# Raw edge blocks and source numbers fetched ahead of the gathers, kept in DRAM and brought back by SyncE

## What is computed

```python
edge_index = stack([src, dst])                  # 200,000 edges + one loop a node, sorted by dst
x = x + gnn(layernorm(x), edge_index, W, b, prelu_a)
x = x + ffn(layernorm(x)[None], Wr, br, W1, b1, W2, b2, gamma, beta)[0]

def gnn(x, edge_index, k_centers, W, b, prelu_a):
    deg = segment_sum(ones, dst); dinv = rsqrt(deg)
    h = x @ W
    out = segment_sum(h[src] * (dinv[src] * dinv[dst])[:, None], dst) + b
    return where(out > 0, out, prelu_a * out)
# ffn: 8 experts, the two best chosen once from the mean over all nodes, then for every node
#      gelu(x @ W1[e] + b1[e]) @ W2[e] + b2[e], weighted sum of the two, + x, layer norm
```

## Time and profile before

| | us |
|---|---|
| median of 3 runs | 1024.82 (1023.86 to 1029.19) |
| the profiled execution | 1025.88 |
| span of its core | 1024.4 |
| mean granted TensorE clock | 0.987 |

### The profile page before, as it was taken

How to read it: one execution, slowest core, us unless ns; L and a number is a source line. 1 busy time by engine, 2 the same in 40 slices (tenths; PEclk the granted TensorE clock), 3 DMA queues, 4 the chain that set the end, 5 groups by cost and what they waited for, 6 DMA issues and landing times.

```text
span 1024.4 us, 20188 instructions
## 1 busy us (share of the span) xinstructions
PE 981.2 (96%) x6916; PEld 831.5 (81%) x6917; DVE 845.5 (83%) x1737; ACT 508.5 (50%) x998; POOL 550.8 (54%) x510
## 2 busy tenths in 40 slices
PE   8899999999999999999997997989899999999996
PEld 7677788888888788888885876878799999999996
DVE  6988888889999899998984977966777887878786
ACT  6585444444444444444442443433764647474641
POOL 4074288788887888878887887842001111111111
PEclk9999999999999999999998998999999999999998
DMA  9059847656657566676655765656201111111101
GB/s 304 24 131 271 141 121 164 156 140 149 151 144 167 140 162 148 151 166 152 149 139 145 174 152 144 156 127 232 74 32 47 47 46 46 46 46 46 46 21 36
DMA packets 68512, 126.37 MB, mean 123 GB/s; under 512 B 10084, under 2 KB 49262, under 8 KB 68430
## 3 DMA queue, kind: packets, MB, share of 16 engines
q0 software_dynamic: 32448, 90.88, 38.0%
q1 hardware_dynamic: 35982, 34.40, 10.6%
HBM read 68.12 MB, written 25.67 MB: 92 GB/s over the span
## 4 chain that ended last, share of the span: by engine, by line
PE 47%; POOL 28%; issue 9%; DMA 7%; DVE 6%; ACT 2%; DVEq 0%; ACTq 0%; POOLq 0%; SPq 0%
POOL fetched L815 19%; PE banks L2005 13%; PE banks L2116 13%; PE banks L2130 8%; DMA partial<-fetched 4%; PE banks L2135 4%; PE banks L1981 3%; POOL partial L815 3%; POOL partial L828 3%; PE banks L1843 3%; POOL raw L755 2%; DMA partial<-h_rows,node_row 1%; POOL extra_row L785 1%; DVE hot_src L1012 1%; DVE hot_key L1012 1%
## 5 line engine op out<-in xcount | busy, mean ns | idle before, releaser
L2005 PE MATMUL banks<-tab,adj 128*128 128x512 f32 x2009 | 505.4, 401 | 1.3 <-ACT adj L1725 1.3
L2005 PEld LDWEIGHTS banks<-tab,adj 128*128 128x128 f32 x2009 | 369.2, 190 | 73.9 <-DVE tab L1129 1.5
L1720 ACT CAST adj<-banks 128x784 fp32r<-128x784 f32 x320 | 247.9, 817 | 347.2 <-PE banks L1981 319.2
L815 POOL DMA_INDIRECT fetched<-h_rows,node_row x240 | 313.3, 1305 | 78.3 <-issue 68.0
L1012 DVE TENSOR_TENSOR hot_src<-iota_src,turned 128x2048 bf16<-128x2048 bf16 x164 | 199.9, 1219 | 37.0 <-PE banks L1981 29.5
L1981 PEld LDWEIGHTS banks<-hot_key,hot_src 128*128 128x128 bf16 x2560 | 124.8, 98 | 56.4 <-issue 31.2
L1981 PE MATMUL banks<-hot_key,hot_src 128*128 128x98 bf16 x2560 | 149.0, 210 | 14.5 <-DVE hot_key L1012 13.2
L1012 DVE TENSOR_TENSOR hot_key<-iota_key,turned 128x1568 bf16<-128x1568 bf16 x164 | 158.8, 968 | 0.0
L2130 PE MATMUL banks<-W2s,gh 128*128 128x512 f32 x384 | 137.4, 399 | 0.6 <-DVE pre L1538 0.6
L1771 ACT ACTIVATE gh<-banks,b1e 128x384 fp32r<-128x384 f32 (+1 forms) x136 | 78.3, 576 | 88.9 <-PE banks L2116 88.7
L2135 PE MATMUL banks<-W2s,gl 128*128 128x256 f32 x392 | 110.0, 281 | 0.0
(11 more groups left out here) (259 smaller groups left out, 1148.1 us busy)
## 6 DMA issues: line engine op xcount, KB each, us to landing
partial<-fetched POOLq DMA_DIRECT2D x48, 640.0 KB
xin<-in_x SPq DMA_DIRECT2D x49, 128.0 KB
x_dram<-x SPq DMA_DIRECT2D x49, 128.0 KB
x1f<-x_dram POOLq DMA_DIRECT2D x16, 384.0 KB, 3.8
out<-res SPq DMA_DIRECT2D x48, 128.0 KB, 1.7
h_rows<-tab SPq DMA_DIRECT2D x5, 1024.0 KB, 15.2
h_rows<-tab POOLq DMA_DIRECT2D x5, 1024.0 KB
W1a<-in_W POOLq DMA_DIRECT2D x8, 512.0 KB, 5.7
```

Source lines behind the costliest of these rows:

```text
L815: g.indirect_dma_start(out=into, out_offset=None, in_=h_rows, in_offset=bass.IndirectOffsetOnAxis(ap=node_row[:, m, r:r + 1], axis=0), bou ...
L1720: s.copy(adj[k][:, :].rearrange("p (q n) -> p q n", n=P)[:, :, at:at + 2 * BANK_NODES].rearrange("p q (b n) -> p q b n", b=2), bank_pairs[ ...
L2005: last = mm(acc[k][:, :], adj[k][:, q * P:(q + 1) * P], tab[:, q, :], start=(at == 0), stop=(at == T - 1), skip_group_check=True)
```

## The change

- Of the 21 raw blocks the first three (`DIRECT`) are fetched as before. The other 18 are fetched by GpSimd in three batches of six (`BATCHED`) into a new buffer, `staging`, of six blocks. It lies over the end of the room that `fetched` takes later. SyncE stores each into a DRAM tensor, `staged` (`keep_staged`). All of this stands ahead of the first round: one batch before the first two parts of `add_low_rows`, one behind them, one behind the last two. SyncE's `keep_staged` stands before its first `xin` loads, between the third and the fourth store of `h_rows`, and behind the sixth.
- In the second stage SyncE brings raw block 3, 4, ... from `staged` into `raw`, behind the output store and the `xin` load of every second dense block.
- All 8 lists of source numbers are fetched ahead of `add_low_rows`, straight into `node_row`, where `node_rows` rewrites them in place. `node_rows(m)` for m of 2 and more moves to `rows_of(m + 1)`.
- GpSimd's second stage is left with rounds, `add_group` and `load_extra_rows`. There is no pace by dense blocks any more; the first round that writes `fetched` waits for all 18 stores, and the wait for the extra source numbers moves to the first `load_extra_rows`.
- The first gathered block is 9 instead of 10; the other seven stay.
- For the last gathered block `add_partials` moves behind the next `hot_step`.
- The list of gathered blocks now has two even runs, so some small operations of the first stage come in two pieces.

Core of the diff:

```diff
-GFIRST, GCYCLE = 10, 5
-FETCH_FROM, PACE = 2, 8
+GFIRST, GCYCLE = 9, 5
+DIRECT, BATCHED = 3, 6
...
-    GATHERED = list(range(GFIRST, T - 3, GCYCLE))
+    GATHERED = [GFIRST] + list(range(GFIRST + GCYCLE + 1, T - 3, GCYCLE))
...
+    STAGED = [range(at, min(at + BATCHED, NP)) for at in range(DIRECT, NP, BATCHED)]
...
     def rows_listed_at(m):
-        return 2 * m - 2
+        return m + 1
...
             with sp.If(is_dense(sp)):
+                def keep_staged(b):
+
+                    sp.wait_ge(raw_staged, (b + 1) * 16 * BATCHED)
+                    for i, q in enumerate(STAGED[b]):
+                        sp.dma_start(staged[q], staging[:, i, :]).then_inc(raw_kept, 16)
+
+                keep_staged(0)
                 for d in range(2):
                     sp.dma_start(xin[:, d, :], x[d * P:(d + 1) * P, :]).then_inc(tile_by_sp[d], 16)
...
                     sp.dma_start(h_rows[lo * P:hi * P, :].rearrange("(t p) d -> p t d", p=P), tab[:, lo:hi, 0:D].bitcast(F32)).then_inc(hi_stored[i // 2], 16)
+                    if i == 2:
+                        keep_staged(1)
+                keep_staged(2)
                 for d in range(T):
                     sp.wait_ge(epi, d * EPI + (2 * EPI + 5))
                     sp.dma_start(x1_dram[d * P:(d + 1) * P, :], x1[:, d % 2, :]).then_inc(x1_by_sp[d % 2], 16)
                     if d + 2 < T:
                         sp.dma_start(xin[:, d % 2, :], x[(d + 2) * P:(d + 3) * P, :]).then_inc(tile_by_sp[d % 2], 16)
+                    q = DIRECT + DENSE.index(d) // 2 if d in DENSE and DENSE.index(d) % 2 == 0 else NP
+                    if q < NP:
+                        if q == DIRECT:
+                            sp.wait_ge(raw_kept, (NP - DIRECT) * 16)
+                        sp.wait_ge(raw_free, q + 1)
+                        sp.dma_start(raw[:, q % 2, :, :].rearrange("r p s -> r (p s)"), staged[q]).then_inc(raw_back[q % 2], 16)
...
+                def stage_edges(q):
+
+                    g.indirect_dma_start(
+                        out=staging[:, (q - DIRECT) % BATCHED, :], out_offset=None,
...
+                        in_offset=bass.IndirectOffsetOnAxis(ap=starts[:, q:q + 1], axis=1),
+                        bounds_check=last_edge).then_inc(raw_staged, 16)
...
                         n = group_number(m, group)
+                        if n == 0 and r % WIDE == 0:
+                            pool.wait_ge(raw_kept, 48 * BATCHED)
...
-                for i in range(ND):
-                    if i % 2 and i + 5 < ND:
-                        load_edges((i + 5) // 2)
-                    for m in range(2, NGATH):
-                        if i == rows_listed_at(m):
-                            load_node_src(m)
-                    for m, r in rounds(i):
+                for m in range(NGATH):
+                    for r in range(SUMMED):
                         fetch_round(m, r)
                         if r // WIDE > 1 and r % WIDE == 1:
                             add_group(m, r // WIDE - 1)
                         if r == 2 and m:
                             add_group(m - 1, GROUPS - 1)
-                        if r == SUMMED - 1:
-                            load_extra_rows(m)
+                    load_extra_rows(m)
                 add_group(NGATH - 1, GROUPS - 1)
...
-                    dve.wait_ge(raw_in[k], q // 2 * 16 + 16)
+                    if q < DIRECT:
+                        dve.wait_ge(raw_in[k], q // 2 * 16 + 16)
+                    else:
+                        dve.wait_ge(raw_back[k], (q - DIRECT) // 2 * 16 + 16)
...
                     if beside:
+                        if m == NGATH - 1:
+                            add_partials(m)
                         add_extra(m)
...
-                        if b == rows_listed_at(m) + 3:
+                        if b == rows_listed_at(m):
                             node_rows(m)
-                    if DENSE[b - 1] - 1 in GATHERED:
+                    if DENSE[b - 1] - 1 in GATHERED[:NGATH - 1]:
                         add_partials(GATHERED.index(DENSE[b - 1] - 1))
```

76 lines of the change are left out of this document (44 added, 32 removed).

## The result

| | before | changed |
|---|---|---|
| median, us | 1025.90 (1023.86 to 1029.19, 4 runs) | 1009.73 (1009.26 to 1014.92, 4 runs) |
| the profiled execution, us | 1025.88 | 1009.26 |
| span of its core, us | 1024.4 | 1007.8 |
| mean granted TensorE clock | 0.987 | 0.991 |

The ratio is 0.985, interval 0.981 to 0.989: 16.2 us faster. On two further chips it was 0.979 (0.976 to 0.983) and 0.984 (0.979 to 0.988). Ratios leave out executions more than 1.5% above the fastest of their kernel, which concerns only the run `e2_adds_first`.

The account below looks back on a forecast made before the run. GpSimd's queue was taken to bound the second stage's end; of 23.6 us lost 4.5 stay, so span 1024.4 - 19.1 + 0.3 = 1005.6, median 1006 us. Forecast range 1001 to 1013; 8 times in 10, 1000.5 to 1014.5.

Parts of the forecast that it names:

- What bounded the kernel: End of second stage: GpSimd's queue, 69 us per gathered block against about 59.3 us of dense work, bounds it.
- The end of the rounds: Second stage on GpSimd: last round ends at 132 + 528 = 660 us instead of 676.5.
- First round: GpSimd, end of first stage: issued at 132 us, 9 later than before; bounds 124 and 137.
- The rounds: GpSimd's second stage: 518.6 us without raw blocks and lists, plus 5.6 and 4 us of corrections, take 528 us.
- The 5.6 us for a VectorE that waits less: GpSimd's rounds: 25.4 us of VectorE waits lay within them; without these the same work takes 5.6 us more.
- The cover of `xin`: Early second stage: x of block 2 lands at 138, VectorE adds it at 140.49, so covered by 2.5 us.
- the prediction's own last sentence: Forecast wrong if rounds' mean exceeds 1.4 us, first round after 140, or VectorE waits for xin or raw block at 140 to 145.
- What stays lost: Last gathered blocks, second stage: 3.8 + 0.2 us and half a us of lower clock, 4.5 of the 23.6 us lost before.
- All of it: Rival, second stage: last round ends before 656, the whole 23.6 us come back, 1001.3 us; chance 0.2.
- The pace is the DMAs': Rival, GpSimd's rounds: they slow to fill the room raw blocks leave; gain about 3, 1022 us; chance 0.09.
- The head start is lost: Rival, before the rounds: first round at 155, 27.5 us lost instead of 23.6, 1029 us; chance 0.05.
- Group waits: Rival, GpSimd's rounds: some 40 groups wait 0.55 us over the 0.3; 17 us stay lost, 1018.5 us; chance 0.1.

Follow-up runs that it names:

- e2_adds_first: Changed kernel with the second eight extra_src DMAs moved behind the adds 4 and 5 and the third batch; ratio 0.994 (0.989 to 0.999).

## Why the prediction was right, step by step

**What bounded the kernel** was right: the raw blocks alone, put back among the rounds, bring the old time back.

**The end of the rounds** was forecast at 660 and is 660.8. That it came out to the us is luck: two errors of opposite sign, 5.7 us late at the start and 4.8 us short behind it.

- *First round*: 132 forecast, 137.67 measured. Batch one (landed 63, measured 62.87), the first `h_rows` store (66, measured 67.1), the adds 0 and 1 (75, measured 77.0), SyncE's second stores (95, measured 94.65) and the adds 2 and 3 (103, measured 104.2) came nearly as summed. The price of a piece was too low: staged blocks and `extra_src` took 1.26 and 1.41 us of writing and 0.30 to the next, with single ones up to 2.6, against "some 1.45" in all for a staged block, so the adds 4 and 5 went at 120.9 instead of 118; and from there it took until 137.67, 16.8 us for two adds beside the third batch, where the forecast had 7.2 each. As a ledger of GpSimd from its last direct raw block to the first round: 31.6 us more of writing (66.2 instead of 34.6) and 22 more gaps of 0.30 are 38.2 us; of the 31.4 us of idle time that was there, 7.1 are left. That makes 13.9 of the 14.4 us.
- *The rounds*: 528 forecast, 523.2 measured. The group waits are right to the tenth: 15.2 us in 19 pieces, less 0.3 each, are 9.5 us instead of 5.5, so 4.0 more; the tenth is luck, since the changed kernel on another chip has 12.7 in 18, which is 1.8 more. The 5.6 us for a VectorE that waits less didn't come: the mean round is 1272 ns instead of 1305. The correction took the price as one for time in which VectorE works. By the ends of the rounds it is paid for each pair of one-hot operations, and their number is nearly the same: 145 pairs of them started between the first and the last round before and 139 now, with 0.53 and 0.51 us beyond the 1.01 of a round for each pair. Besides, the means of the profiles here go from 1265 to 1322 ns at full width, 14 us over 240 rounds, and the three with no VectorE wait for sums or `x` at all have 1287, 1302 and 1302. A correction of 5.6 us is under that wander.

**The cover of `xin`** is the step that failed: "covered by 2.5 us". The third batch was put down as landing at 133, 1 us behind the adds, and "hidden" in GpSimd's 20 us wait. In the changed kernel GpSimd's wait is gone (3.4 us), filled by pieces put before it; the batch ends at 134.3 and landed at 139.5, 5.2 us behind its last piece. The load of `x` was put down with 1.7 us, the landing time of an output store of the third stage; it took 4.7. What I took from before as free room had already been spent on the lists, batches and `extra_src` of my own sum. By the prediction's own last sentence a wait for `xin` at 140 to 145 would have shown the forecast wrong; it came (138.3 to 147.6), cost 8.3 us early, and the time still is 1009.7 and not 1018. The sentence before saved it: "such an early loss also moves the places at which the late sums are needed". The repeat with the stores later shows that as measured. So the time came out right although this step was wrong.

**What stays lost**: 4.5 us forecast, 11.0 measured. The end of the last round was right, but not where the rounds of the block before it would end: 67.6 us earlier by the forecast, 63.3 measured (597.5), since the last block's rounds were the quickest of all (mean 1195 ns). Its sum came 13.2 us behind that, at 610.69, instead of at 604.6. So the late place is block 41, by 2.7 us, and block 46 has none, where the forecast had 3.8. If the early 8.3 us hadn't been, some 9 would have been lost late instead, as the edited kernel shows (9.2). So the 6.5 us that stay lost beyond the forecast aren't put down to the early wait but to the sum at block 41, 6.1 us later than forecast. Of the 6.5 us, 0.7 were there to lose besides the 23.6, 1.8 came back in the first stage of this profile, 0.8 at block 18, 0.7 in the third stage, and the 0.3 put for small things didn't show: that leaves the 2.2 us between the spans, 1005.6 and 1007.8. The other 1.5 us between 1006 and 1009.7 are the step from span to median: the profiled execution was 1.1 us above the median before, and is 0.5 below it now.

**The rivals.** "All of it" didn't come true, as first round and group waits took their share. "The pace is the DMAs'" fell with the half rows. That rounds are slowed by VectorE is shown by their ends, 0.89 us behind the end of the one-hot operation in which they were issued. The rule of the Trainium skill (SBUF — State Buffer, "SBUF: two separate sides") that the prediction leaned on, ports held for a whole instruction, has that shape. But for writing descriptors the section names copies, casts and tensor-scalar operations, and it infers that tensor-tensor operations, which the one-hot operations here are, don't hold it up. The 18 group adds agree with that, the 127 rounds don't. Another rule of the same section, that a VectorE instruction with two SBUF inputs contends with a GpSimd instruction that reads SBUF, would tell the two apart, since a round reads its row list and an add reads none. No run here tests which port it is. "The head start is lost" was the nearest: 5.7 us of the 19 that it needed, and the edits on the order of adds and batches moved the first round by no more than 4 us forward. "Group waits" stayed at the 4 us of the sum, in another profile at 1.8.

## What to carry to other kernels

When work is moved ahead into an engine's idle stretch, fill the stretch once in the ledger: pieces with their mean price in that stage, then whatever waits behind them on the queue that serves two masters; here 38 us of pieces met 31 us of idle time, and the rest showed up as a late load on another engine's queue. Where a chain with a fixed rate ends the stage, losses ahead of its last deadlines don't add up, so mending an early wait gave nothing that could be measured; look for what moves the chain's end. And before shortening one queue, follow the other that meets it: 27 us less on GpSimd gave 3.5. A mean price that wanders is worth laying beside the other engines' rows: here it splits into 1.09 and 1.48 us by what VectorE was in when the piece was issued.

## What the runs showed that was not expected

- On one chip the first stage ended late in each of four profiles (93.95, 102.3, 103.1 and 106.7 us against 85.3 to 90.6 on the others), with waits of 3 to 11 us that name no work on ScalarE, VectorE and TensorE. The kernel before took 1026.51 us on that chip, no more than elsewhere, and two of the edited kernels 1020. That the kernel before hides the delay because its second stage ends by GpSimd is argued and not shown: it wasn't profiled there. What disturbs the first stage is open.
- GpSimd's time for an indirect DMA doesn't follow its bytes: 1272 ns at 1 KB a row, 1327 at 512 B. It follows VectorE: a round issued inside a bf16 tensor-tensor operation of 0.97 or 1.22 us ends 0.89 us behind that operation's end (median of the 127 such rounds of 280 in the changed kernel). Group adds issued inside such operations aren't held (0.97 to 1.04 us). The accumulating add of half rows costs 1654 ns on GpSimd and 1010 for whole rows.
- The mean of the same 240 rounds varies from 1265 to 1303 ns between three profiles of the same kernel, and a block's from 1.195 to 1.344 us within one; so the end of 523 us of such work can't be forecast to better than some 5 us.
